# Attention in one fused layer: two heads' scores in the two halves of TensorE's rows, in float32r parts, and row maxima of two heads by one VectorE instruction

## The chip, the cores and the metric

The kernel runs on one core of a Trainium2 chip. The metric is the device time of one execution in microseconds (us). The profiler's record of one execution is a span from its first to its last instruction.

## The reference

One layer with gated cross-attention and a gated mixture of experts, all in float32, with B=4, S=512, D=256, 16 heads of 16, 8 experts of which each token takes 2, and a shared expert of width 512:

```
q = split_heads(layernorm(x) @ Wq.T + bq);  k, v = split_heads(ctx @ Wk.T + bk), split_heads(ctx @ Wv.T + bv)
attn = softmax(einsum('bhqd,bhkd->bhqk', q, k) / 4)
x = x + tanh(g_xattn) * (merge_heads(einsum('bhqk,bhkd->bhqd', attn, v)) @ Wo.T + bo)
x = x + tanh(g_ffn) * (moe(layernorm(x)) + (silu(h @ gate_w) * (h @ up_w)) @ down_w)
```

## The kernel before, in words

The program is written engine by engine: each engine's block is a list of instructions in program order, with semaphores between the engines. Nothing reorders them.

**Projections.** For each batch `b`, TensorE makes the value rows (`value_rows`) and four tiles of 128x512 of k and q (`chunk(b, j)`; j 0 and 1 are k, 2 and 3 are q). A score needs more digits than a bf16 product has, so every tile of q and k is cut into three bf16 parts: ScalarE writes the first (`first_part`), VectorE the float32 remainder (`rest`), ScalarE the second part (`second_part`), GpSimd the third (`third_part`). SyncE stores the parts in DRAM (`store_parts`) and loads them back (`load_group`) so that the 16 rows of a head stand six times above each other, as the six pairs of parts in `Q_PART` and `K_PART`: 96 partitions of QS (queries) and KST (keys) for one head, four heads side by side. A bf16 product over these 96 rows sums the six partial products.

**Groups.** Four heads of a batch are a group; there are 16 groups (`GROUPS`), each of four steps `kt` (a tile of 128 keys). A step of group i has on TensorE, in this order: scores of heads 0 and 1 (L1523, keys in the partitions, queries along 512 columns), one product for the maxima (L1305, `scores_for_max`, queries in the partitions), scores of head 2, a second product for the maxima, in step 2 the transpose of the finished maxima (`max_transpose`, L1315), the product with the values of the step before (`values`, L1395: four heads in four column tiles of 32, two instructions each), a third product for the maxima, scores of head 3, a fourth product for the maxima. The maxima run six heads ahead (`smax_schedule`); they end with step 1 of group 14. In the last six steps pieces of the output projection and of the next stage (`tail`) stand at the end of each step.

**The softmax.** exp needs minus the row maximum, which is added by the score product itself: rows 96 and 97 of QS hold minus the maximum in two bf16 parts, the same rows of KST hold ones (a GpSimd memset for each b, `kones`). VectorE takes each 128x512 product's maxima (L842, `one_max`), TensorE turns the 128x16 tile into PSUM bank 7, ScalarE copies the first part (`m_first`, L676), VectorE subtracts for the second (`m_second`, L853), and two DMAs bring them into QS (`load_max`, L360). ScalarE applies exp to each score tile (L730) and, once a group, copies the group's output (`out_copy`, L718).

**PSUM.** Banks 0 to 2 are the ring of the scores, 3 to 5 the ring of the maxima, 6 holds the output, 7 the turned maxima and a bias product. A score product waits until exp has read the bank three tiles before; a maxima product waits for the reduction three tiles before.

**SyncE.** In group i it loads the first four of the six terms of group i+3 (8 DMAs, after the scores of group i-1), the maxima of group i+1 (2 DMAs), the other two terms (4 DMAs), and three small transfers of softmax sums and scales.

Of the kernel before, what the change touches and what calls it, by code (L numbers as in the profile page):

```python
# [5 lines left out]
P = 128  # L6
# [4 lines left out]
BF16 = mybir.dt.bfloat16  # L11
# [4 lines left out]
def flamingo_layer(nc, x, ctxT, g_xattn, g_ffn, WqT, bq, WkT, bk, WvT, bv, WoT, bo,  # L16
# [16 lines left out]
    TERMS = 6  # L33
    Q_PART = [0, 1, 2, 0, 1, 0]
    K_PART = [0, 0, 0, 1, 1, 2]
# [18 lines left out]
    q_scr = nc.dram_tensor("q_parts", (B, 3, D, S), BF16, kind="Internal").ap()  # L54
    k_scr = nc.dram_tensor("k_parts", (B, 3, D, S), BF16, kind="Internal").ap()
# [9 lines left out]
    with ExitStack() as stack:  # L65
# [6 lines left out]
        def sems(name, n):  # L72
# [30 lines left out]

        R1 = sb("R1", [P, 8192])
# [10 lines left out]
        REST = R3[:, 0:2048].rearrange("p (j n) -> p j n", j=4)  # L115
        QP = R3[:, 5120:8192].bitcast(BF16).rearrange("p (j a n) -> p j a n", j=4, a=3)

        QS = [R1[:, 1024 * g:1024 * (g + 1)].bitcast(BF16).rearrange("p (h n) -> p h n", h=G) for g in range(NG)]
        KST = [R1[:, 4096 + 1024 * g:4096 + 1024 * (g + 1)].bitcast(BF16).rearrange("p (h n) -> p h n", h=G)
               for g in range(NG)]  # L120
# [4 lines left out]
        mparts = sb("mparts", [G * TB, 2, 2, P], BF16)  # L125
# [79 lines left out]
        q1_ready, q2_ready, q3_ready = (sem(n) for n in ("q1_ready", "q2_ready", "q3_ready"))  # L205
        rest_ready = sem("rest_ready")
# [7 lines left out]
        smax_done, max_ready = sem("smax_done"), sem("max_ready")  # L214
        mt_done, m1_ready, m2_ready = sem("mt_done"), sem("m1_ready"), sem("m2_ready")
        m_in = sems("m_in", 2)
        st_done, exp_done, pv_done, ot_ready = sem("st_done"), sem("exp_done"), sem("pv_done"), sem("ot_ready")
# [44 lines left out]

        def smax_schedule(i, kt):

            s = 4 * i + 6 + kt
            return s if s < GROUPS * G else None

        OUT_AT = TB + 1
        M2_AT = 2 * TB + 1
# [11 lines left out]
        def bank(kind, b, part=0):  # L281
            return 3 + USERS.index((kind, b, part)) % 3

        def gu_bank(n, k):
# [4 lines left out]
            return (2, 6)[k] if n < IC + 2 else 2 + k  # L289
# [7 lines left out]
        def smax_bank(n):  # L297
# [4 lines left out]
            return (6, 4, 5)[n % 3] if n < EARLY else 3 + n % 3  # L302

        def max_user(n):

            users = [m for m in range(n) if smax_bank(m) == smax_bank(n)]
            return users[-1] + 1 if users else 0
# [12 lines left out]
        def _(sp):  # L320
# [14 lines left out]
            def store_parts(b):  # L335
                for j in range(4):
                    dst = k_scr if j < 2 else q_scr
                    sp.wait_ge(q3_ready, 4 * b + j + 1)
# [7 lines left out]
            def load_group(i, terms=range(TERMS)):  # L346
# [1423 lines left out]
```

## Time and profile before

| | us |
|---|---|
| median of 3 executions | 469.4 (468.83 to 470.41) |
| span of the profiled execution | 466.8 |
| TensorE busy in it | 453.6 (97%) |
| VectorE busy | 331.8 (71%) |
| ScalarE busy | 252.6 (54%) |
| GpSimd busy | 154.4 (33%) |

The profiled execution's own time isn't given apart from its span. Busy time of TensorE is modelled and counts a product until its end has drained, so a product that follows another closely overlaps it in the rows: what a product takes of a stream is read from the distance of two starts, not from its duration. PE is TensorE's matmul, PEld its weight load, DVE is VectorE, ACT ScalarE, POOL GpSimd, SPq the DMA queue of SyncE. The tensors R1 to R4 appear as R, PSUM as PS.

### The profile page before, as it was taken

The page shows a single profiled execution, that of the slowest core. Times are in us where ns is not written, and L with a number is a line of the kernel's source. Part 1 is how long each engine was busy: PE and PEld are TensorE (multiplying, and loading weights), DVE is VectorE, ACT ScalarE, POOL GpSimd, SP SyncE. Part 2 cuts the span into 40 slices and gives each one's busy share as a digit, 9 for nine tenths or more (in the row PEclk, how much of TensorE's full clock was granted, in tenths as well). Part 3 has the DMA queues.
Part 4 walks back from the last instruction along what each step waited for, and adds up shares of the span by engine and source line. Part 5 has one row for each costly group of instructions (what it writes and reads, how often), then busy time and mean ns, then how long its engine had stood idle before and what let it go on. Part 6 is the DMA issues. An engine that isn't in the chain of part 4 may idle for free.

```text
span 466.8 us, 8100 instructions
## 1 busy us (share of the span) xinstructions
PE 453.6 (97%) x2310; PEld 215.8 (46%) x2310; DVE 331.8 (71%) x841; ACT 252.6 (54%) x540; POOL 154.4 (33%) x209
## 2 busy tenths in 40 slices
PE   8999999999999999999999989889999999999997
PEld 8664432222222222222465634565555555555745
DVE  1988898888888888888578766354565656532674
ACT  2664477777777777777565111023666766631110
POOL 5493488111212121212132766600323332332000
PEclk9999999999999999999999999979999999999999
DMA  8669762335353535353548522311322222312921
GB/s 261 223 181 251 157 204 58 86 83 97 90 98 94 98 94 97 95 92 102 167 135 264 211 91 81 110 48 46 93 84 88 85 88 83 90 49 60 377 101 47
DMA packets 54140, 56.71 MB, mean 121 GB/s; under 512 B 13456, under 2 KB 44560, under 8 KB 54096
## 3 DMA queue, kind: packets, MB, share of 16 engines
q1 hardware_dynamic: 47504, 43.82, 34.1%
q0 software_dynamic: 4960, 10.53, 7.4%
q10 hardware_dynamic: 1632, 1.84, 1.2%
q8 instruction: 20, 0.33, 0.3%
q14 instruction: 24, 0.20, 0.2%
HBM read 36.35 MB, written 17.72 MB: 116 GB/s over the span
## 4 chain that ended last, share of the span: by engine, by line
PE 90%; DVE 4%; issue 2%; DMA 1%; SPq 1%; another core or an unknown queue 1%; POOL 1%; ACT 1%; DVEq 0%; POOLq 0%
PE PS L1395 13%; PE PS L1305 13%; PE PS L1523 12%; PE PS L1567 11%; PE PS L1677 9%; PE PS L1580 6%; PE PS L1696 5%; PE PS L1357 4%; PE PS L1672 3%; PE PS L1442 3%; PE PS L1691 2%; PE PS L1651 2%; DVE nmax L842 2%; PE PS L1335 2%; PE PS L1659 2%
## 5 line engine op out<-in xcount | busy, mean ns | idle before, releaser
L842 DVE TENSOR_REDUCE nmax<-PS 128x1 f32<-128x512 f32 x256 | 159.4, 683 | 21.4 <-PE PS L1305 21.4
L730 ACT ACTIVATE R<-PS 128x512 f32<-128x512 f32 x256 | 134.1, 601 | 42.0 <-PE PS L1523 41.7
L1305 PE MATMUL PS<-R 96*128 96x512 bf16 x256 | 96.1, 382 | 1.2 <-DMA R<-k_parts 1.0
L1523 PE MATMUL PS<-R 98*128 98x512 bf16 x256 | 86.2, 380 | 0.3 <-DVE R L860 0.3
L1395 PE MATMUL PS<-R 128*32 128x512 f32 x512 | 68.2, 604 | 0.0
L621 POOL DMA_INDIRECT token_y<-R,dest x34 | 32.6, 960 | 93.4 <-DVE R L1184 92.0
L1305 PEld LDWEIGHTS PS<-R 96*128 96x128 bf16 x256 | 24.8, 97 | 69.7 <-DVE nmax L842 51.1
L1677 PE MATMUL PS<-R 128*128 x100 | 47.3, 595 | 0.2 <-ACT R L798 0.2
L745 ACT ACTIVATE R<-PS 128x512 f32<-128x512 f32 x16 | 9.6, 597 | 68.7 <-PE PS L1567 52.1
L600 POOL DMA_DIRECT2D CH<-R x56 | 27.4, 496 | 54.4 <-ACT R L718 54.4
L1523 PEld LDWEIGHTS PS<-R 98*128 98x128 bf16 x256 | 24.8, 97 | 38.6 <-ACT R L730 22.6
L1222 DVE TENSOR_TENSOR R<-R,PS 128x256 f32<-128x256 f32 x34 | 14.3, 421 | 33.3 <-issue 19.7
L575 POOL DMA_INDIRECT slot_x<-CH,pos x32 | 31.1, 972 | 13.7 <-issue 8.7
L568 POOL TENSOR_TENSOR CH<-CH,w_v 128x512 f32<-128x512 f32 x7 | 8.9, 1265 | 77.7 <-DMA w_v<-o_scales 77.7
L1567 PE MATMUL PS<-R,wup 128*128 128x512 f32 x64 | 32.0, 625 | 1.5 <-issue 1.5
L1567 PE MATMUL PS<-R,wgate 128*128 128x512 f32 x64 | 30.7, 596 | 2.0 <-issue 2.0
L1580 PE MATMUL PS<-wdown,R 128*128 128x256 f32 x128 | 29.7, 388 | 0.0
L795 ACT ACTIVATE R<-PS 128x256 f32<-128x256 f32 x34 | 13.0, 383 | 29.7 <-PE PS L1677 26.3
L1580 PEld LDWEIGHTS PS<-wdown,R 128*128 128x128 f32 x128 | 24.8, 196 | 5.2 <-issue 2.0
L1696 PE MATMUL PS<-fc,R 128*128 x100 | 25.6, 380 | 0.0
L1677 PEld LDWEIGHTS PS<-R 128*128 128x128 f32 x100 | 18.7, 190 | 14.3 <-issue 13.1
L533 POOL TENSOR_TENSOR R<-R 128x512 bf16<-128x512 f32 x16 | 18.5, 1160 | 18.2 <-ACT R L669 18.1
(177 smaller groups left out, 598.4 us busy)
## 6 DMA issues: line engine op xcount, KB each, us to landing
R<-q_parts SPq DMA_DIRECT2D x96, 64.0 KB, 3.1
R<-k_parts SPq DMA_DIRECT2D x96, 64.0 KB, 3.1
R<-in_fc_w_dram SPq DMA_DIRECT2D x16, 256.0 KB
R<-token_y SPq DMA_DIRECT2D x4, 1024.0 KB, 9.0
R<-slot_x SPq DMA_DIRECT2D x25, 129.0 KB
k_parts<-R SPq DMA_DIRECT2D x8, 384.0 KB, 3.3
q_parts<-R SPq DMA_DIRECT2D x8, 384.0 KB, 3.5
fc<-in_fc_w_dram SPq DMA_DIRECT2D x16, 128.0 KB
```

The source lines that it names most:

```text
L575: nc.gpsimd.indirect_dma_start(slot_x, bass.IndirectOffsetOnAxis(ap=pos[:, t, k:k + 1], axis=0), CH[:, t, :], None).then_inc(scattered, 16)
L600: pool.dma_start(CTX[at:at + DK, i // 2, :], OT[i % 2][P // G * j:P // G * j + DK, :]).then_inc(ctx_in[i % 2], 16)
L621: nc.gpsimd.indirect_dma_start(token_y, bass.IndirectOffsetOnAxis(ap=dest[:, j:j + 1], axis=0), YE[:, j % UN, :], None).then_inc(y_out[j % ...
L730: nc.scalar.activation(PT[:, kt, j, :], PS[:, (G * (TB * i + kt) + j) % 3, :], ACT.Exp).then_inc(exp_done, 1)
L842: nc.vector.tensor_reduce(nmax[:, i % 2, j * TB + qt:j * TB + qt + 1], PS[:, smax_bank(n), :], AX.X, ALU.max, negate=True).then_inc(max_re ...
L1305: mm(PS[:, smax_bank(n), :], QS[g][0:KS, j, qt * P:(qt + 1) * P], KST[g][0:KS, j, :], start=True, stop=True).then_inc(smax_done, 1)
L1395: last = mm(PS[32 * j:32 * j + VW, 6, :], VA[:, b * TB + kt, (g * G + j) * VS:(g * G + j) * VS + VW], PT[:, kt, j, :], start=(kt == 0), st ...
L1523: mm(PS[:, n % 3, :], KST[g][0:KM, j, kt * P:(kt + 1) * P], QS[g][0:KM, j, :], start=True, stop=True).then_inc(st_done, 1)
L1567: last = mm(PS[:, gu_bank(n, k), :], w[:, d, c * P:(c + 1) * P], H2T[:, d, b * S:(b + 1) * S], start=(d == 0), stop=(d == DC - 1))
L1580: last = mm(PS[:, down_bank(b, t), half * D:(half + 1) * D], HS[:, b % 2, c, t * P:(t + 1) * P], wdown[:, c, :], start=(c == 0 and half == ...
L1677: last = mm(PS[:, 1 + u, :], XGT[:, u, c * P:(c + 1) * P], fc1[:, c, e, :], start=(c == 0), stop=(c == DC - 1))
L1696: last = mm(PS[:, 5 + u, 0:D], HET[:, u, c * P:(c + 1) * P], fc2[:, c, e, :], start=(c == 0), stop=(c == IE // P - 1))
```

## The change

1. **Parts.** q and k are cut into two parts in place of three: the high part is rounded to float32r by ScalarE, the low part is the float32 remainder that VectorE writes at once. `second_part` and `third_part` go. Three pairs of parts (high-high, low-high, high-low) in place of six: 48 rows for one head, 50 with the two rows of maxima, and both operands are float32r.
2. **Halves.** Heads 0 and 2 of a group stand in partitions 0 to 49, heads 1 and 3 in 64 to 113. A product takes one of the two halves of the rows.
3. **Maxima.** The products for the maxima alternate between the halves and use banks 4 to 7 in pairs; one VectorE instruction reduces two banks (128x2x512) to two columns. The first 24 are still reduced one by one.
4. **Turned maxima.** VectorE splits the 128x16 maxima before the transpose (`split_max`, two small instructions); TensorE turns both parts at once into a bank of the scores' ring (turn 11 of a group's 17), and ScalarE copies them out with one instruction (`max_rows`), after the exp of step 2, head 2. Both DMAs of `load_max` follow it.
5. **Order.** In a step: scores 0 and 1, maxima 0 and 1, scores 2, transpose, values, scores 3, maxima 2 and 3. Output bank 6 becomes 3; later users of 3 to 5 take 4 to 6.
6. The ones in KST are whole-tile memsets at the start, and a group's loads wait for them. `bias_row` stands before VectorE's first step.

```
-    TERMS = 6
-    Q_PART = [0, 1, 2, 0, 1, 0]
-    K_PART = [0, 0, 0, 1, 1, 2]
+    TERMS = 3
+    Q_PART = [0, 1, 0]
+    K_PART = [0, 0, 1]
+    UNIT = 2 * TERMS
+    HALF = P // 2
...
-    q_scr = nc.dram_tensor("q_parts", (B, 3, D, S), BF16, kind="Internal").ap()
+    q_scr = nc.dram_tensor("q_parts", (B, 2, D, S), F32, kind="Internal").ap()
...
+        MT_AT = 2 * G + 3
+        def score_turn(i, kt, j):
+            return (G * TB + 1) * i + G * kt + j + (i + 1 < GROUPS and G * kt + j >= MT_AT)
+        def max_turn(i):
+            return (G * TB + 1) * (i - 1) + MT_AT
...
-            return (6, 4, 5)[n % 3] if n < EARLY else 3 + n % 3
+            return (6, 4, 5)[n % 3] if n < EARLY else 4 + (n - EARLY) % 4
...
-            def load_group(i, terms=range(TERMS)):
+            def load_group(i, pieces=range(UNIT)):
...
+                else:
+                    sp.wait_ge(kones, g + 1)
...
+                for piece in pieces:
+                    t, r = divmod(piece, 2)
+                    at = slice(HALF * r + t * DK, HALF * r + (t + 1) * DK)
+                    sp.dma_start(QS[g][at, :, :].bitcast(F32),
+                                 q_scr[b, Q_PART[t], rows, :].rearrange("(h r d) n -> r d h n", r=2, d=DK)[r])\
+                      .then_inc(ld_group[g], 16)
...
             def load_max(i):
-                for part, s in ((0, m1_ready), (1, m2_ready)):
-                    sp.wait_ge(s, i + 1)
+                sp.wait_ge(m_ready, i + 1)
+                for part in range(2):
+                    sp.dma_start(QS[i % NG][KS + part:P:HALF, :, :].bitcast(F32).rearrange("p h n -> p (h n)"),
+                                 mparts[G * TB * part:G * TB * (part + 1), i % 2, :]).then_inc(m_in[i % 2], 16)
...
+            def two_max(n):
+                i, _, at = max_tile(n)
+                for r in range(2):
+                    dve.wait_ge(smax_done[r], n // 2 + 1)
+                nc.vector.tensor_reduce(nmax[:, i % 2, at:G * TB:G * TB // 2], PS[:, smax_bank(n):smax_bank(n) + 2, :], AX.X,
+                                        ALU.max, negate=True).then_inc(max_ready, 1)
+            def split_max(i):
+                dve.wait_ge(max_ready, maxima(G * TB * (i + 1)))
...
+                nc.vector.tensor_copy(nmax_parts[:, i % 2, 0, :].bitcast(F32R), nmax[:, i % 2, :]).then_inc(high_max, 1)
+                dve.wait_ge(high_max, i + 1)
+                nc.vector.tensor_tensor(nmax_parts[:, i % 2, 1, :], nmax[:, i % 2, :], nmax_parts[:, i % 2, 0, :],
+                                        ALU.subtract).then_inc(split_ready, 1)
...
+            bias_row()
             for i in range(GROUPS):
                 for kt in range(TB):
...
+                    t = smax_schedule(i, kt)
+                    for h in range(2):
+                        if t is not None:
+                            two_max(TB * t + 2 * h)
+                        if kt == 1 and h == 1 and i + 1 < GROUPS:
+                            split_max(i + 1)
...
             def max_transpose(i):
+                pe.wait_ge(split_ready, i + 1)
+                if i:
+                    turn_free(max_turn(i))
...
-                    mm(PS[:, n % 3, :], KST[g][0:KM, j, kt * P:(kt + 1) * P], QS[g][0:KM, j, :],
-                       start=True, stop=True).then_inc(st_done, 1)
+                    turn = score_turn(i, kt, j)
+                    turn_free(turn)
+                    h, r = divmod(j, 2)
+                    at = slice(HALF * r, HALF * r + KM)
+                    mm(PS[:, turn % 3, :], KST[g][at, h, kt * P:(kt + 1) * P], QS[g][at, h, :],
+                       start=True, stop=True).then_inc(st_done[r], 1)
...
                     mx[0]()
+                    mx[1]()
                     scores(kt, 2)
-                    mx[1]()
...
+                    scores(kt, 3)
                     mx[2]()
-                    scores(kt, 3)
                     mx[3]()
```

## Rows read from the trace of the kernel before

**Rows 1.** Chain that ended last, the page: shares of the span.
```profile
PE 90%; DVE 4%; issue 2%; DMA 1%; SPq 1%; another core or an unknown queue 1%; POOL 1%; ACT 1%; DVEq 0%; POOLq 0%
```
**Rows 2.** Busy time by stretch: stretch, length, busy (count) by engine, clock, DMA, GB/s.
```profile
139.90:151.40 11.50, 11.50 (x69) 3.23 (x65) 10.27 (x19) 8.89 (x18) 3.19 (x5) 1.00 0.38 91
```
**Rows 3.** Timeline, one step of group 6: start, us, engine, line, what [idle before].
```profile
140.15 0.38 PE L1523 MATMUL PS<-R 98*128 98x512 bf16 x1
...
140.35 2.48 DVE L842 TENSOR_REDUCE nmax<-PS 128x1 f32<-128x512 f32 x4 [0.36 <-PE PS L1305]
140.37 0.38 PE L1305 MATMUL PS<-R 96*128 96x512 bf16 x1
...
140.57 2.06 ACT L730 ACTIVATE R<-PS 128x512 f32<-128x512 f32 x4 [0.78 <-PE PS L1523]
...
141.22 0.10 PEld L1523 LDWEIGHTS PS<-R 98*128 98x128 bf16 x1 [0.31 <-ACT R L730]
...
141.46 0.38 PE L1305 MATMUL PS<-R 96*128 96x512 bf16 x1
...
141.77 1.06 PE L1395 MATMUL PS<-R 128*32 128x512 f32 x8
...
142.77 0.39 PE L1305 MATMUL PS<-R 96*128 96x512 bf16 x1
```
**Rows 4.** Timeline, the values' product one group later.
```profile
153.28 1.07 PE L1395 MATMUL PS<-R 128*32 128x512 f32 x8
```
**Rows 5.** Groups of instructions, whole span: busy, mean ns | idle before, releasers.
```profile
L842 DVE TENSOR_REDUCE nmax<-PS 128x1 f32<-128x512 f32 x256 | 159.4, 683 | 21.4 <-PE PS L1305 21.4
L730 ACT ACTIVATE R<-PS 128x512 f32<-128x512 f32 x256 | 134.1, 601 | 42.0 <-PE PS L1523 41.7
L1184 DVE COPY R<-PS 128x256 f32<-128x256 f32 x34 | 14.4, 424 | 11.7 <-PE PS L1696 7.2 <-PE PS L1691 2.8
L955 DVE COPY R<-PS 128x512 f32<-128x512 f32 x4 | 2.7, 686 | 2.0 <-remote 1.9
L1017 DVE TENSOR_TENSOR PRE<-PRE,OHS 128x8 f32<-128x8 f32 x16 | 2.7, 167 | 0.5
```
**Rows 6.** Timeline of SyncE's queue, one round of DMA issues.
```profile
153.60 0.46 SPq L352 DMA_DIRECT2D R<-q_parts  x1
...
159.48 1.29 SPq L360 DMA_DIRECT2D R<-mparts  x2
...
164.06 0.58 SPq L376 DMA_DIRECT2D w_v<-o_scales  x1
```
**Rows 7.** DMA issues: count, size, median us to landing.
```profile
R<-mparts SPq DMA_DIRECT2D x32, 4.0 KB, 2.3
```
**Rows 8.** Timeline of TensorE ahead of the first group.
```profile
16.76 3.70 PE L1357 MATMUL PS<-R,w_q 128*128 128x512 f32 x8
20.30 1.04 PE L1282 MATMUL PS<-ident,R 128*128 128x128 f32 x8
...
36.95 0.61 PE L1305 MATMUL PS<-R 96*128 96x512 bf16 x2 [0.98 <-DMA R<-k_parts]
...
53.62 0.27 PE L1315 MATMUL PS<-ident,nmax 128*16 128x128 f32 x1
```
**Rows 9.** Timeline of VectorE, ScalarE and GpSimd around the first group's start.
```profile
59.66 0.74 DVE L860 SCALAR_TENSOR_TENSOR R<-PS,bias_sc,R 128x512 f32<-128x512 f32 x1
60.44 0.62 ACT L669 CAST R<-R 128x512 bf16<-128x512 f32 x1 [1.00 <-DVE R L860]
62.38 0.93 POOL L551 TENSOR_SCALAR tg_bo<-bo_row,tg 128x256 f32<-128x256 f32 x1
```
**Rows 10.** Timeline of TensorE in one of the last six steps.
```profile
236.50 0.81 PE L1523 MATMUL PS<-R 98*128 98x512 bf16 x3
237.25 1.06 PE L1395 MATMUL PS<-R 128*32 128x512 f32 x8
```

More of the change, by code:

```diff
@@ L10 @@
 F32 = mybir.dt.float32
-BF16 = mybir.dt.bfloat16
+F32R = mybir.dt.float32r
 U32 = mybir.dt.uint32
@@ L101, in flamingo_layer @@
         minus_half = sb("minus_half", [P, NT])
+        with nc.sbuf_tensor("QK", [P, 8192], F32R) as QK:
+            pass
         R1 = sb("R1", [P, 8192])
@@ L261, in flamingo_layer, with max_tile, maxima @@
         EARLY_J = ((0, 0, 0, 0), (0, 0, 0, 0), (2, 2, 2, 2), (2, 2, 2, 2))
+        def max_tile(n):
+            i, m = divmod(n, G * TB)
+            h, m = divmod(m, 2 * TB)
+            qt, r = m // 2, m % 2
+            return i, (h, r, qt), 2 * TB * r + TB * h + qt
+        def maxima(tiles):
+            return min(tiles, EARLY) + max(tiles - EARLY, 0) // 2
+        MT_AT = 2 * G + 3
[3 more added lines that the diff above has]
+            return (G * TB + 1) * (i - 1) + MT_AT
         def smax_schedule(i, kt):
@@ L288, in gu_bank @@
                 return k
-            return (2, 6)[k] if n < IC + 2 else 2 + k
+            return 2 + k
         def down_bank(b, t):
@@ L675, in m_first @@
                     act.wait_ge(m_in[i % 2], 32 * (i // 2))
-                nc.scalar.copy(mparts[:, i % 2, 0, :], PS[0:G * TB, 7, 0:P]).then_inc(m1_ready, 1)
+                nc.scalar.copy(mparts[:, i % 2, :], PS[0:2 * G * TB, max_turn(i) % 3 if i else 7, 0:P]).then_inc(m_ready, 1)
             def load_context(b):
@@ L893, in _ @@
                 for j in range(4):
-                    if b == B - 1 and j == 2:
-                        m_second(0)
+                    if b == B - 1 and j == 1:
+                        split_max(0)
                     early_max(EARLY_J[b][j])
@@ L898, in _ @@
             early_max(EARLY - sum(map(sum, EARLY_V + EARLY_J)))
-            def head_max(s):
-                for qt in range(TB):
-                    one_max(TB * s + qt)
             def scale_of(i):
@@ L953, in h2t_second @@
                 dve.wait_ge(h2_t, 2 * b + 2)
-                dve.wait_ge(st_done, G * TB * (GROUPS - 1 + b // 2))
+                for r in range(2):
+                    dve.wait_ge(st_done[r], G // 2 * TB * (GROUPS - 1 + b // 2))
                 nc.vector.tensor_copy(H2T[:, 1, b * S:(b + 1) * S], PS[:, bank("h2_t", b, 1), :]).then_inc(h2t_ready[1], 1)
```

203 lines of the change are left out of this document (82 added, 121 removed).

## Prediction

> **What bounds the kernel now.** I read first the chain that ended last: 90% of it is TensorE [rows 1]. The busy table of one group (11.50 us, four steps) shows TensorE without a gap, VectorE at 10.27 us, ScalarE at 8.89 us, at the full granted clock of 2.4 GHz [rows 2]. So in groups 0 to 14 a step takes what TensorE's stream takes. The timeline has the parts: a bf16 product follows the next after 0.22 us (140.15, 140.37), the values start 0.31 us after the last product before them (141.46 to 141.77), and the next product 1.00 us after they start (to 142.77) [rows 3]. Eight products and the values: 7 x 0.22 + 0.31 + 0.99 = 2.84 us. Four such steps and the transpose (0.14 more) are 11.51 us, the distance of two values' products a group apart (141.77, 153.28) [rows 3, 4]. VectorE has 0.36 us idle a step, ScalarE 0.78 us [rows 3]: neither is far behind.
>
> **The products.** A float32r product isn't in the trace. Its bounds: a bf16 one costs 0.22 us of the stream [rows 3]; a float32 one of 512 columns stands as two instructions of 0.44 us each (eight from 16.76 to 20.30) [rows 8], 0.88 us in all, four times the bf16 price, as of four narrow partial products. One product of parts that are already narrow is one of these four: I take 0.22 us; 0.44 us (float32 operands streamed as slowly as there) and 0.88 us are the ends. Weight loads don't hold it up: float32 loads of 128 columns keep a pace of 0.11 us with their products ((1.04 - 0.28) / 7) [rows 8], and two loads stand to one 0.22 us of a pair.
>
> That two halves of the rows work side by side isn't in the trace either. Its nearest row is the values: eight instructions of column tiles, which end to end would be 8 x 0.44 = 3.5 us, take 1.00 us [rows 3, 8]. Bounds for a pair: 0.22 us (side by side) and 0.44 us (one after the other). I take side by side. In the new order every two neighbours are of different halves, or the third follows in the half that comes free, so eight products take 4 x 0.22 = 0.88 us where they took 1.75 us. TensorE's own work in a step falls from 2.84 to about 2.0 us. That isn't the new step: TensorE waits in program order, and the other limits are near.
>
> A switch between the values' column tiles and whole rows costs the trace little: 0.09 us before the values (0.31 - 0.22) and 0.14 us after them (1.00 less two passes of 0.43) [rows 3]; the new order has the same two switches a step and one more at the transpose. TensorEngine Tiling in the Trainium skill (Key Properties) says that a change of tiling mode drains the engine, and that speaks against this change, whose products are in a third mode. By that rule the sum would be the drain rival's below; by the row it stays as it is.
>
> **The new step.** The products of step kt, the values of kt-1 and exp form a ring. After the values only scores 3 can start; head 2 of the next step uses the bank of scores 3, and the next values need its exp. So: values 0.99, scores 3 to the start of exp 0.42 (140.15 to 140.57), exp 0.58 (its four take 2.06, at 0.49 from start to start), 0.07 to TensorE (the first exp ends 141.15, the load starts 141.22), scores 2 and the switch 0.31 [rows 3]: 2.37 us. In place of 2.84 us, and set by latencies, not by work.
>
> VectorE: a reduction of 512 columns takes 0.683 us, 0.60 from start to start ((2.48 - 0.68) / 3) [rows 3, 5]. Copies from PSUM of 256 and 512 columns (424 and 686 ns) give 1.02 ns a column [rows 5], so 1024 columns take 0.68 + 0.52 = 1.21 us, 1.13 from start to start, 2.26 us a step against 4 x 0.60 = 2.40 now. It fits under 2.37 us, and `two_max` alone gains little. ScalarE: 4 x 0.49 = 1.96 us a step. Once a group `out_copy` comes ahead of the exp of step 0, head 3: it can start only when the last values have ended, takes 0.50 us, and pushes that exp by about 0.22 us.
>
> **The wait that the change adds.** `split_max` needs all sixteen maxima of the next group, the last of which come from the second pair of step 1. From the start (0) of that step's values: maxima 3 is issued at 1.21 us, can be read at 1.63, VectorE reads it until 2.84, then its two small instructions, which wait for the one before each: 2 x 0.17 (nearest row, 128x8 columns) + 0.08 = 0.42 us [rows 5]. TensorE may transpose at 3.33 us and starts the next values at 3.64 us, 1.27 us later than 2.37. Before, the transpose needed one reduction less and no split, and lay in 0.14 us. Behind the waiting transpose on TensorE stand the values and scores 3; exp runs dry meanwhile. The transpose also takes a turn of the ring, and ScalarE copies 128 columns in 0.25 us or less, behind an exp: no further cost that I can see.
>
> Group: 4 x 2.37 + 0.22 + 1.27 = 10.97 us, against 11.51: **-0.54 us**. Over groups 0 to 13 and half of 14: 14.5 x -0.54 = **-7.8 us**.
>
> **The transfers.** SyncE issues 17 DMAs a group, 12 of them loads of the same number and size. It is at it from 153.60 to 164.64 us with a pause only ahead of the maxima (157.4 to 159.48) [rows 6]: 9.0 us of 10.97, no bound. The maxima's DMAs are issued behind exp and copy, about 1.4 us after the transpose, and land 0.6 + 2.3 = 2.9 us later [rows 6, 7], 4.3 us after it; the next group's scores come a step, the values and the rest after it: also about 4.3 us. Taken as nothing; 0.3 us a group (4 us in all) if it lands late.
>
> **Ahead of the groups.** The chain to the first loads loses ScalarE's and GpSimd's parts, some 1.8 us, so the wait of 0.98 us at 36.95 goes; ten pairs of early maxima could save 0.22 us each; the first transpose (53.62), issued at once before, waits for a split, 0.5 us [rows 8]. Between -0.98 - 2.2 + 0.5 = -2.7 and 0; since VectorE and the banks wait for each other there, I take **-1.5 us**. Stores grow from 384 to 512 KB; nothing waits for them but the reuse of QP. `bias_row` now stands ahead of VectorE's first pair and waits for tanh and GpSimd's 0.93 us, which come after the last part of q: VectorE is free at about 59.7, ready at 60.2 [rows 9]: **+0.5 us**.
>
> **The last six steps** are TensorE's work (out projection): scores 0 to 2 took 0.22 each (236.50, 0.81 for three with the end, then values at 237.25) [rows 10]; one of them falls beside another: 6 x -0.22 = **-1.3 us**. What follows shifts with it.
>
> **Sum:** -7.8 - 1.5 + 0.5 - 1.3 = -10.1 us. The profiled span of 466.8 us becomes 456.7; the median lies 2.6 us above that span, so the time is **459.3 us**. Split at 0.17 or 0.7 us, side costs of 0.3 us a group and the early bounds give 450 to 468 for this case.
>
> **The rivals.**
> - *Forecast* (halves side by side at 0.22 us): 0.60.
> - *No wait at the transpose.* If VectorE isn't late, the 1.27 us shrink to the transpose's 0.3 us: 14.5 x -0.97 = -14, 445 us. Against it: the order of the instructions. 0.07.
> - *The halves don't run side by side (the other side).* Then TensorE's work stays 2.84 us a step, and the new order adds the split's wait at the transpose, 0.83 us more a group than now (I follow the same chain with 0.22 us for each product: 12.34 us): 14.5 x 0.83 = +12, and none of the early and late savings: 481 us. It decides once a pair takes over about 0.3 us in place of 0.22. For it: no row of the trace shows row tiles; against it: the column tiles. 0.13.
> - *Half rate,* 0.44 us a product side by side: 12.48 us a group, 483 us; TensorE is then as full as before. 0.07. FP8 and Floating Point Precision in the Trainium skill (TensorE Precision Notes) names four passes for float32 and one read of reduced precision beside it, which speaks against; no row here shows it.
> - *Full price,* 0.88 us: over 18 us a group, 570 us. 0.03.
> - *Drains.* If each switch with the half-row mode costs 0.1 us more, nine a group, group 11.8 us: +0.3 x 14.5 = +4, less the early and late 2.3: 471 us. The page's rule; the switches in the trace are against it. 0.08.
> - Anything else (a late load, the clock falling in the new waits): 0.02.
>
> **How the numbers follow.** Faster is the forecast, the first rival and the edge of the drains; no measurement of this kernel tells less than 0.3% from no change. Faster 0.68, same 0.05, slower 0.27. The forecast's own range is 450 to 468; to hold 8 in 10 it has to reach over the drains to the edge of the serial halves: 448 to 481.
>
> **What the next profile would show.** Two products of one pair starting within some tens of ns, 0.22 us between pairs; `two_max` at 1.21 us; values 2.4 us apart in plain steps and 3.6 us around the transpose; the transpose's weight load idle some 1 us behind the split; the first score of a group not waiting for `mparts`; groups at 11.0 us. Starts 0.22 us apart within a pair, or a duration of 0.6 us for a product, make it wrong.

## The result, and the profile after

The changed kernel takes 482.8 us (median of 4 runs, 479.4 to 489.3) where the kernel before takes 469.1 us (467.0 to 470.4) on the same chip: a ratio of 1.028, 95% interval 1.022 to 1.034. **It is slower.** The prediction was 459.3 us, 448 to 481: wrong in sign, and the time lies outside the range. Ratios in this document leave out runs more than 1.5% above the fastest of their kernel, which had a lower granted clock (here the one of 489.3 us); medians hold all runs. The profiled execution took 481.0 us, with a span of 479.3 against 466.8.

The page of the kernel after: the busy shares, the granted clock in 40 slices, the chain (its line for before is in [rows 1]), and two groups of instructions.
```profile
PE 449.7 (94%) x2310; PEld 231.2 (48%) x2310; DVE 326.5 (68%) x741; ACT 246.7 (51%) x524; POOL 132.4 (28%) x193
...
PEclk9999988999999999999989999989999999999999
...
PE 80%; DVE 10%; issue 3%; ACT 2%; DMA 2%; another core or an unknown queue 1%; POOL 0%; ACTq 0%; DVEq 0%; POOLq 0%
...
L865 DVE TENSOR_REDUCE nmax<-PS 128x2 f32<-128x1024 f32 x116 | 137.9, 1221 | 26.1 <-PE PS L1320 26.1
...
L1548 PEld LDWEIGHTS PS<-QK 50*128 50x128 f32 x256 | 42.6, 188 | 80.9 <-ACT R L742 61.9
```
TensorE's share of the chain fell from 90% to 80% and VectorE's rose from 4% to 10%: TensorE waits for VectorE now.

The timeline of the step ahead of the transpose and of the transpose itself, one group of the kernel after; [rows 3] is the step of before.
```profile
140.75 1.06 PE L1418 MATMUL PS<-R 128*32 128x512 f32 x8
...
141.75 0.18 PEld L1548 LDWEIGHTS PS<-QK 50*128 50x128 f32 x1 [0.84 <-ACT R L742]
141.75 0.49 PE L1548 MATMUL PS<-QK 50*128 50x512 f32 x1
...
141.75 0.73 PE L1320 MATMUL PS<-QK 48*128 48x512 f32 x2
...
142.28 2.06 ACT L742 ACTIVATE R<-PS 128x512 f32<-128x512 f32 x4 [0.53 <-PE PS L1548]
...
142.59 1.23 DVE L865 TENSOR_REDUCE nmax<-PS 128x2 f32<-128x1024 f32 x1 [0.18 <-PE PS L1320]
...
143.85 0.17 DVE L873 CAST nmax_parts<-nmax 128x16 fp32r<-128x16 f32 x1
144.05 0.17 DVE L875 TENSOR_TENSOR nmax_parts<-nmax,nmax_parts 128x16 f32<-128x16 f32 x1
...
144.28 0.28 PE L1337 MATMUL PS<-ident,nmax_parts 128*32 128x128 f32 x1 [0.87 <-DVE nmax_parts L875]
...
144.50 1.07 PE L1418 MATMUL PS<-R 128*32 128x512 f32 x8
```
The halves do run side by side: scores 3 and a maxima product both start at 141.75. But exp starts 0.53 us behind the scores (forecast 0.42), and the plain steps that follow, values at 144.50, 147.10 and so on, are 2.61 us long where 2.37 was forecast. The transpose waits 0.87 us; from the values at 140.75 to those at 144.50 it is 3.75 us (forecast 3.64). Three plain steps, 0.07 for `out_copy` and 3.75 make 11.65 us, against 11.51 before.

Some groups are longer. Timeline of the kernel after beside GpSimd's scaling of the context:
```profile
154.88 1.26 POOL L588 TENSOR_TENSOR CH<-CH,w_v 128x512 f32<-128x512 f32 x1 [12.90 <-DMA w_v<-o_scales]
155.50 0.67 DVE L873 CAST nmax_parts<-nmax 128x16 fp32r<-128x16 f32 x1
...
156.43 0.28 PE L1337 MATMUL PS<-ident,nmax_parts 128*32 128x128 f32 x1 [1.35 <-DVE nmax_parts L875]
```
The cast takes 0.67 us instead of 0.17, and TensorE waits for all of it. The first split inside the loop meets other work of GpSimd, additions of 128x256 tiles from 64.55 to 75.56 us, and both of its instructions are slow:
```profile
70.81 0.67 DVE L873 CAST nmax_parts<-nmax 128x16 fp32r<-128x16 f32 x1
71.52 0.65 DVE L875 TENSOR_TENSOR nmax_parts<-nmax,nmax_parts 128x16 f32<-128x16 f32 x1
```
And TensorE's clock falls to the lower of its two levels where it did not before. Busy time by stretch (columns as in [rows 2]), kernel after; then one of these stretches in the kernel before:
```profile
62.00:66.00 4.00, 3.04 (x14) 1.21 (x12) 3.73 (x7) 2.59 (x5) 2.77 (x12) 1.00 0.67 230
66.00:70.00 4.00, 4.00 (x19) 1.83 (x19) 2.58 (x3) 2.21 (x5) 4.00 (x6) 0.61 1.01 365
70.00:74.00 4.00, 2.23 (x15) 0.72 (x15) 3.23 (x4) 1.38 (x4) 4.00 (x7) 0.93 0.04 14
74.00:78.00 4.00, 4.00 (x22) 1.65 (x19) 2.36 (x2) 2.31 (x5) 1.56 (x3) 0.61 0.02 4
```
```profile
66.00:70.00 4.00, 3.85 (x25) 1.19 (x27) 3.70 (x8) 3.06 (x8) 3.78 (x9) 1.00 0.93 311
```
A granted clock of 0.61 over 4 us is mostly 1.2 GHz. TensorE had waited (busy 3.04 of 4 us) ahead of it.

**Where 12.5 us of span went**, by the starts of values in both timelines: the first values come at 66.58 instead of 63.77 (+2.8); those behind the first transpose of the loop at 72.43 instead of 67.03 (+2.6 more); 14 groups later 239.50 instead of 228.13 (+6.0: 14 x 0.14 = 2.0, four slow splits beside GpSimd 2.6, and 1.2 in the first of these groups, part of which ran at half clock); the last values at 268.36 instead of 253.52 (+3.5); after them 210.9 us instead of 213.3 (-2.3; from 300 to 330 us the granted clock is 0.94 instead of 0.89).

### The profile page after: what moved, and what is told of

It is laid out like the page before. It is cut to its first block, busy times and chain, and to the rows that moved or that the text cites. A ratio compares the mean times of both kernels' runs of the same rounds, so it can differ in the third digit from the quotient of the medians.

```text
span 479.3 us, 8092 instructions
## 1 busy us (share of the span) xinstructions
PE 449.7 (94%) x2310; PEld 231.2 (48%) x2310; DVE 326.5 (68%) x741; ACT 246.7 (51%) x524; POOL 132.4 (28%) x193
## 4 chain that ended last, share of the span: by engine, by line
PE 80%; DVE 10%; issue 3%; ACT 2%; DMA 2%; another core or an unknown queue 1%; POOL 0%; ACTq 0%; DVEq 0%; POOLq 0%
PE PS L1418 14%; PE PS L1590 12%; PE PS L1548 11%; PE PS L1700 9%; PE PS L1603 6%; PE PS L1320 5%; PE PS L1719 5%; DVE nmax L865 4%; PE PS L1380 3%; PE PS L1465 3%; PE PS L1695 3%; ACT R L742 2%; PE PS L1714 2%; PE PS L1674 2%; DMA X<-in_x_dram 2%
## 5 line engine op out<-in xcount | busy, mean ns | idle before, releaser
L865 DVE TENSOR_REDUCE nmax<-PS 128x2 f32<-128x1024 f32 x116 | 137.9, 1221 | 26.1 <-PE PS L1320 26.1
L1548 PE MATMUL PS<-QK 50*128 50x512 f32 x256 | 94.2, 455 | 1.8 <-ACT R L742 0.5
L1548 PEld LDWEIGHTS PS<-QK 50*128 50x128 f32 x256 | 42.6, 188 | 80.9 <-ACT R L742 61.9
L1320 PE MATMUL PS<-QK 48*128 48x512 f32 x256 | 78.3, 449 | 0.4 <-DVE nmax L865 0.2
L1418 PE MATMUL PS<-R 128*32 128x512 f32 x512 | 69.6, 616 | 0.0
L1320 PEld LDWEIGHTS PS<-QK 48*128 48x128 f32 x256 | 34.6, 187 | 13.8 <-DVE nmax L851 5.4
L794 ACT COPY R<-R 128x512 f32 x36 | 20.7, 629 | 4.7 <-issue 4.7
```

What stands on the lines that cost most here:

```text
L865: nc.vector.tensor_reduce(nmax[:, i % 2, at:G * TB:G * TB // 2], PS[:, smax_bank(n):smax_bank(n) + 2, :], AX.X, ALU.max, negate=True).then ...
L1320: mm(PS[:, smax_bank(n), :], QS[g][at, h, qt * P:(qt + 1) * P], KST[g][at, h, :], start=True, stop=True).then_inc(smax_done[n % 2], 1)
L1418: last = mm(PS[32 * j:32 * j + VW, 3, :], VA[:, b * TB + kt, (g * G + j) * VS:(g * G + j) * VS + VW], PT[:, kt, j, :], start=(kt == 0), st ...
L1548: mm(PS[:, turn % 3, :], KST[g][at, h, kt * P:(kt + 1) * P], QS[g][at, h, :], start=True, stop=True).then_inc(st_done[r], 1)
```

## The experiments

Chips differ: before took 469.0, 459.6, 468.2 and 471.1 us in the four sessions. So each time is read against before in its own session.

**1. Products alone.** The layer is left out; TensorE runs series of ten products of each kind, and the output is not the layer's.
```
for _ in range(10):
    mm(PS[:, 0, :], FR[0:96, 0:P], FR[0:96, 512:1024]); values()       # L73, the float32 values L67
...
for _ in range(10):
    mm(PS[:, 0, :], BF[0:50, 0:P], BF[0:50, 512:1024])                 # L113
    mm(PS[:, 5, :], FF[:, 0:P], FF[:, 512:1024])                       # L114, a whole float32 product
```


> Leaves the whole layer out: it only issues series of TensorE products on the same tiles and writes a part of x as output. Each series is ten rounds. Values means the kernel's product with the values (four column tiles of 32, float32, 512 columns), 0.99 to 1.00 us of the stream. One product in front of the values, round by round: bf16 over 96 rows 1.31 us (the trace of before). Theory A (the cost is in the switch to a tile of 64 rows: the engine drains and cannot load ahead): float32r over 96 rows also 1.31 to 1.35, bf16 over 50 rows and float32r over 50 rows both about 1.53. Theory B (the cost is in float32r, whose weights are not loaded ahead): float32r over 96 rows and over 50 rows both about 1.53, bf16 over 50 rows 1.31. Streams: bf16 and float32r over 96 rows 0.22 us a product, halves of the rows in turn 0.11 us a product, float32r on one half alone 0.22. Between whole float32 products of 0.86 us: bf16 over 96 rows adds 0.22, a 50-row product adds 0.41 (early part of the changed kernel) by theory A whatever its type. Eight float32r products in the two halves and the values: 0.88 + 1.0 + 0.2 to 0.3 = 2.1 to 2.2 us; eight bf16 products and the values 2.84.

Timeline of TensorE in this kernel: bfloat16 of 96 rows between values; float32r of 96; bfloat16 of 50 rows; last, float32r pairs of two halves.
```profile
15.44 0.39 PE L69 MATMUL PS<-BF 96*128 96x512 bf16 x1
...
16.76 0.39 PE L69 MATMUL PS<-BF 96*128 96x512 bf16 x1
...
33.12 0.50 PE L73 MATMUL PS<-FR 96*128 96x512 f32 x1
...
34.55 0.50 PE L73 MATMUL PS<-FR 96*128 96x512 f32 x1
...
43.32 0.39 PE L77 MATMUL PS<-BF 50*128 50x512 bf16 x1
...
44.64 0.39 PE L77 MATMUL PS<-BF 50*128 50x512 bf16 x1
...
83.66 0.39 PE L97 MATMUL PS<-FR 50*128 50x512 f32 x1
83.66 0.39 PE L98 MATMUL PS<-FR 50*128 50x512 f32 x1
83.89 0.39 PE L97 MATMUL PS<-FR 50*128 50x512 f32 x1
```
The period with the values is 1.32 us (16.76 - 15.44), 1.43 and 1.32, and 1.43 for float32r of 50 rows. What costs 0.11 us is float32r, not the half rows (theory B, with half of its 0.22 us); and the record of such a product is 0.50 us long instead of 0.39. In a stream float32r keeps 0.23 us a product and a pair of halves takes the same 0.23 (83.66 to 83.89): it is only at the start behind another kind that a product is late. Between whole float32 products it is otherwise. The same kernel, lines 105, 109, 113 and 117 beside whole float32 products:
```profile
90.83 0.38 PE L105 MATMUL PS<-BF 96*128 96x512 bf16 x1
...
91.90 0.38 PE L105 MATMUL PS<-BF 96*128 96x512 bf16 x1
...
113.37 0.39 PE L113 MATMUL PS<-BF 50*128 50x512 bf16 x1
...
114.74 0.39 PE L113 MATMUL PS<-BF 50*128 50x512 bf16 x1
...
127.44 0.50 PE L117 MATMUL PS<-FR 50*128 50x512 f32 x1
...
128.92 0.49 PE L117 MATMUL PS<-FR 50*128 50x512 f32 x1
```
1.07 us with 96 rows, 1.37 with 50, 1.48 with 50 in float32r (float32r of 96 rows: 1.09). Here the half-row tile costs 0.30 us (0.39 in float32r), as theory A has it. And eight float32r products in the two halves with the values take 2.12 us a round, eight bfloat16 products of 96 rows with the values 2.83: TensorE's own work does fall as forecast.

**2. Parts cut to bfloat16.** The products of scores and maxima read the upper 16 bits of each part, so the scores are rounded.
```
-  mm(..., KST[g][at, h, kt * P:(kt + 1) * P], QS[g][at, h, :], ...)
+  mm(..., KST[g][at, h, kt * P:(kt + 1) * P].bitcast(bfloat16)[:, 1:2 * P:2],
+     QS[g][at, h, :].bitcast(bfloat16)[:, 1:2 * S:2], ...)
```


> Edit: the changed kernel, but the products of the scores and of the maxima read the upper 16 bits of each float32 part as bfloat16 (the parts are cut to 8 bits, so the scores are rounded; nothing else is changed, the half rows, the pairs, the reductions and the order stay). Theory (the plain step of 2.61 us is 0.22 longer than forecast because a float32r product that starts behind another kind or behind a wait first shows 0.11 us of its weight load, twice in the ring): the values start 1.00 - 0.11 = 0.89 to 0.91 us ahead of scores 3 or the first exponential starts 0.42 us behind scores 3 instead of 0.53, and scores 2 to values takes 0.31 instead of 0.42, so the plain step is 2.39 us; the transpose step stays at 3.7 us, since VectorE sets it, and a group is 3 x 2.39 + 3.75 = 10.9 us instead of 11.65. Rival (it is the change between half-row tiles and the values' column tiles that costs the time): the plain step stays at 2.61 us and the group at 11.65.

Timeline of one step of this kernel:
```profile
84.78 1.07 PE L1419 MATMUL PS<-R 128*32 128x512 f32 x8
85.78 0.40 PE L1549 MATMUL PS<-QK 50*128 50x512 bf16 x1
...
86.21 2.06 ACT L742 ACTIVATE R<-PS 128x512 f32<-128x512 f32 x4 [0.35 <-PE PS L1549]
...
86.86 0.40 PE L1549 MATMUL PS<-QK 50*128 50x512 bf16 x1
87.19 1.07 PE L1419 MATMUL PS<-R 128*32 128x512 f32 x8
```
Scores 3 to exp 0.43 us (0.53 in the changed kernel), scores 2 to values 0.33 (0.42): the plain step is 2.41 us (84.78 to 87.19), and a group 11.07. The whole takes 461.8 us, one run, where before takes 459.6. So the two terms of the ring that were short are shown, 0.10 us each. The group is 3 x 2.41, 0.19 for `out_copy`, and 3.64 around the transpose; the 0.17 us over the 10.9 expected are `out_copy`, which the expectation had left out. The recorded prediction's group of 10.97 us is met within 0.1 us.

The kernel still isn't faster than before. From its second transpose in the loop to its last (82.15 to 231.12 us) a group takes 11.46 us on average: three splits meet GpSimd's product (the transpose waits 1.68 to 2.00 us), and four groups' first scores wait 0.28 to 0.94 us for the turned maxima.

**3. Transpose behind the values of its step.**
```
                     scores(kt, 2)
-                    if kt == 2 and i + 1 < GROUPS:
-                        max_transpose(i + 1)
                     if kt: values(i, kt - 1) ...
+                    if kt == 2 and i + 1 < GROUPS:
+                        max_transpose(i + 1)
```


> The transpose of the maxima stands behind the values of step 2 in place of ahead of them. My theory (the wait for VectorE's last reduction and the split holds up the values, the ring values, scores 3, exp, scores 2 sets the rest): the values of step 2 start 2.6 us after those of step 1 in place of 3.75, the transpose waits under 0.2 us, a group takes 10.9 us in place of 11.65 (the ring is longer by the transpose, 0.2 to 0.3 us), 14 groups give 10 us: about 472 us. Rival (VectorE is the bound, the wait only shows it): the wait moves to the next maxima products and a group stays above 11.5 us, 480 us or more. Second rival (the maxima's DMAs land too late now that the group is shorter): the first scores of a group wait for the DMA by some 0.5 to 1 us, 478 us.

479.3 us (474.7 to 483.7), 1.020 of before (1.009 to 1.030). The waits at the transpose are gone but for one of 0.20 us, and groups of 10.72 us appear, but in three groups the next scores wait 1.65 to 1.76 us for the turned maxima: the second rival, with a longer wait. Timeline of one group in which they don't wait and the next, in which they do:
```profile
127.08 1.12 SPq L388 DMA_DIRECT2D QK<-mparts  x2
...
129.64 0.64 PE L1548 MATMUL PS<-QK 50*128 50x512 f32 x2
...
137.81 1.12 SPq L388 DMA_DIRECT2D QK<-mparts  x2
...
142.40 0.50 PE L1548 MATMUL PS<-QK 50*128 50x512 f32 x2 [1.65 <-DMA QK<-mparts]
```
The same two transfers landed within 2.6 us of their issue in one group and 4.6 us in the next. Behind one such wait the clock was 0.50 for 12 us and more (190 to 202 us).

**4. The same, and four loads behind the turned maxima's transfers.** In addition to the edit of 3:
```
-  load_group(i + 3, range(0, UNIT - 2)); load_max(i + 1); load_group(i + 3, range(UNIT - 2, UNIT))
+  load_group(i + 3, range(0, UNIT - 4)); load_max(i + 1); load_group(i + 3, range(UNIT - 4, UNIT))
```


> Edit: the changed kernel with the turning of the maxima behind the values of its step (the edit of the run before) and, new, four of each group's loads of parts moved behind the turned maxima's two transfers on SyncE's queue, so that those transfers have no pieces of 64 KB running ahead of them. Theory (in the run before, the turned maxima landed 4.4 us after their issue in every second group, because their 512-byte rows ran in between the pieces still under way, and 2.5 us in the others): no scores product waits for mparts any more, every group but those beside the scaling of the context takes 10.7 us, the span is 475.4 - 5.2 of waits - some 4 us that the lower clock behind one of these waits cost = 466 us, the time about 469 us. Rival (the transfers are late through GpSimd's stores, whatever the order on SyncE): waits of 1.6 to 1.8 us stay in every second group, and the time is that of the run before, 479 us. Second rival (the pieces moved back land too late for the maxima of their group): waits of TensorE for k_parts or q_parts at L1320 appear in most groups, and groups are over 11 us.

**453.2 us (451.7 to 454.5) where before takes 459.6: 0.986 (0.982 to 0.990).** Timeline of this kernel:
```profile
93.46 0.28 PE L1337 MATMUL PS<-ident,nmax_parts 128*32 128x128 f32 x1
...
104.19 0.28 PE L1337 MATMUL PS<-ident,nmax_parts 128*32 128x128 f32 x1
```
From the first transpose in the loop on, groups take 10.72 us, to a few hundredths, those beside GpSimd's scaling too, with no wait of the product for the turned maxima. The gain is shown, though it is under 2%. The span, 451.2 us, isn't to be set against 466.8: this chip is faster, by some 9.5 us for the kernel before.

**5. Again, in five rounds,** without an edit.

> No edit: once more the kernel with the transpose behind the values and four of each group's loads behind the turned maxima's transfers, in five rounds. It took 0.986 of before on a chip on which before took 459.6 us; with the 12 extra products it took 0.991 on a chip on which before took 468.2 us. Theory (the gain is the groups' 0.79 us x 14 = 11 us, less 2.8 us ahead of the groups, 0.7 to 3 in the first group at half clock and 3.2 in the last six steps, and is there on every chip): ratio 0.985 to 0.992 and, in the profile, groups of 10.72 us without a wait for the turned maxima, last values 4 to 6 us sooner than 253.5. Rival (the gain belongs to that one chip): ratio 0.995 or more.

467.1 us (463.7 to 469.8) against 471.1: 0.993 (0.989 to 0.996). The last values start at 249.69 us, 3.8 us sooner than in before; groups are 10.72 us, with some a little longer. Both intervals lie below 1, so the gain doesn't belong to one chip. It came out smaller where the profiled execution had more stretches at the lower clock (mean granted clock 0.978 against 0.996); that the clock is the reason is argued, not shown.

**6. The changed kernel again,** on the chip of the second kernel of experiment 11.

> No edit: the changed kernel once more, on the chip on which the two edits on its queues are compared. Theory (the two edits to the order take 0.93 us from each group and nothing else): this kernel is at 1.02 to 1.033 of before, as in its first comparison, 470 to 474 us where before takes 459.6, and its profile has groups of 11.65 us and more, with a span 16 to 20 us above 451.2: 14 x 0.93 = 13.0 from the groups, some 2.5 to 4 from the casts beside GpSimd's scaling and the rest from stretches of lower clock. Rival (the chip, not the order, made the last kernel fast): this kernel is within 1% of before here.

485.8 us, 1.035 of before (1.030 to 1.040). The rival (within 1% of before) is out, and the ratio lies a little above the 1.02 to 1.033 expected. The chip is not the one of experiment 4: before takes 468.2 us here, so the 470 to 474 us expected can't be compared. Undisturbed groups are 11.65 us again; the granted clock was 0.51 from 68 to 88 us and 0.53 from 184 to 194.

**7. GpSimd scales 8 columns instead of 512** (most of the context goes unscaled): `CTX[:, n, 0:8]` and `SCALES[:, 0:8]`.

> Edit: the changed kernel, but GpSimd scales 8 columns of each context tile instead of 512 (so most of the context goes unscaled). Theory (the casts of the maxima take VectorE 0.67 to 1.18 us instead of 0.17 where GpSimd's 1.26 us product of two SBUF tiles runs at the same time): the groups of 12.15 and 12.6 us go, every undisturbed group is 11.65 us, the transposes wait 0.86 us and none 1.3 or 1.8, and the span falls by about 2.5 to 3 us if nothing else moves. Rival (these casts are late for another reason, for instance DMA traffic): single casts of 0.6 us and more stay and so do the longer groups.

Timeline at the place where the changed kernel's transpose waited 1.35 us:
```profile
154.91 0.20 POOL L588 TENSOR_TENSOR CH<-CH,w_v 128x8 f32<-128x8 f32 x1 [13.82 <-DMA w_v<-o_scales]
155.06 0.28 PE L1337 MATMUL PS<-ident,nmax_parts 128*32 128x128 f32 x1 [0.86 <-DVE nmax_parts L875]
```
Every transpose from the second group of the loop on waits 0.85 to 0.87 us, every one of those groups is 11.65 us but for a few hundredths. GpSimd's product is what lengthened the later splits. The first transpose in the loop still waits 1.77 us, beside GpSimd's additions, which this edit leaves as they are. The single run, 470.0 us, is on the chip on which before takes 459.6: 1.023.

**8. Reductions over half the columns** (the maxima are those of 256 of 512 columns): `PS[:, ...:... + 2, 0:S // 2]`.

> The pair reductions read 256 of each 512 columns, so the maxima are those of half the keys: VectorE's instruction falls from 1.22 to about 0.70 us. My theory (the ring of values, scores, exp and values sets a plain step): plain steps stay at 2.61 us, only the wait at the transpose shrinks by 0.5 us, a group falls from 11.65 to about 11.1. Rival (VectorE's reductions bound the step): four steps of 2 x 0.52 less, a group of 10 us or under.

A reduction takes 0.69 us, the transposes wait 0.33 us instead of 0.87, the plain steps are 2.61 us (values at 95.53 and 98.14), and a group is 11.13 us instead of 11.65. So VectorE bounds the transpose and not the plain step. 476.2 us, one run, on the chip of experiment 3.

**9. Two reductions of one bank in place of one over two banks.**
```
-  tensor_reduce(nmax[... two columns ...], PS[:, bank:bank + 2, :], ...)
+  tensor_reduce(nmax[... first ...], PS[:, bank, :], ...)
+  tensor_reduce(nmax[... second ...], PS[:, bank + 1, :], ...)
```


> Edit: the changed kernel, but two reductions of one bank each (0.68 us each) take the place of one over two banks (1.22). Theory (the reductions do not bound the plain step, but their end sets the transposes' wait): plain steps stay at 2.61 us; the last pair of maxima ahead of the split ends about 0.15 us later in each of the two reductions that follow one another, so the transpose waits 1.0 to 1.2 us instead of 0.86 and a group takes 11.8 to 12.0 us. Rival (VectorE is what holds the plain steps as well): plain steps grow to 2.75 us (four reductions of 0.68) or more, and a group to over 12.2 us.

Timeline: values of the plain steps, and the transpose.
```profile
93.41 1.07 PE L1419 MATMUL PS<-R 128*32 128x512 f32 x8
...
96.02 1.07 PE L1419 MATMUL PS<-R 128*32 128x512 f32 x8
...
102.31 0.09 PEld L1338 LDWEIGHTS PS<-ident,nmax_parts 128*32 128x32 f32 x1 [1.23 <-DVE nmax_parts L876]
102.31 0.28 PE L1338 MATMUL PS<-ident,nmax_parts 128*32 128x128 f32 x1 [0.92 <-ACT R L742]
```
The plain step stays 2.61 us; the transpose waits 0.92 us and a group is 11.72, less than the 11.8 expected. The view names an exp for the product's wait, but the second instruction of the split ends at 102.25 us, and the transpose's own weight load names it. `two_max` gains 0.07 us a group and no more. The single time, 494.0 us, is not read as the edit's price: the granted clock was 0.955 on average (0.50 from 66 to 82 us, where the first transpose waited 4.57 us).

**10. The ones ahead of the first root.** GpSimd's four memsets of K's banks come first, not between its two powers and beside VectorE's normalisation.

> GpSimd writes the ones into the whole KST tiles before its first root instead of behind the second, where VectorE's normalisation of x runs. My theory: the normalisation of batches 1 and 2 takes 1.4 us a batch in place of 2.8, TensorE no longer waits at 26.4 us, and the first values come 0.3 to 0.5 us earlier: 482 us, 0 to 1 us under the changed kernel, which can't be told from no change. The 2.8 us by which the first values came late are in the switches to the half-row tiles between the whole float32 products, which stay. Rival (the late start is the ones' work): all of it goes, 479.5 us.

484.6 us, 1.032 of before (1.025 to 1.038): no gain. The normalisation of four tiles is back at 1.38 us (2.86 in the changed kernel, from 16.94 us, beside memsets from 16.85), yet the first values start 0.8 us later than there (67.42). The traces of the two kernels show where. The first projection product starts at 7.71 us instead of 6.94, a start that lies at 6.79 in experiment 4 and 7.10 in experiment 2, whose instructions are the same up to there; whether the edit has a part in it is not shown. By the transposes of the third batch the lag of 0.77 us is 0.37 (26.80 and 26.43 us; TensorE's wait of 0.23 us for VectorE is gone), so from there the edit gave back 0.4 us, within the 0.3 to 0.5 expected. The lag then stays to the scores (63.19 and 62.84 us), and the other 0.5 us is the clock, granted at 0.76 from 64 to 66 us and 0.50 behind that. So most of VectorE's 1.5 us was not on the path.

**11. Extra products against the lower clock,** alone and with the two edits of 4: each maxima product of the loop's first three steps is issued twice into its bank (12 more products).

> Edit: the changed kernel, but in the first three steps of the group loop each product of the maxima is issued twice into the same bank (12 extra products, no result changed), so that TensorE waits less between 62 and 72 us. Theory (the granted clock of 0.61 and 0.50 between 66 and 78 us follows the stretch in which TensorE was busy only 3.0 of 4 us): with the stretch filled the clock stays at 1.00, values 0 take 1.07 us instead of 1.72, and the transpose of the first group starts 2 to 3 us sooner than at 72.22; span about 2.5 us less. Rival (the clock falls for another reason, such as the transfers of over 300 GB/s in the same 4 us): the clock is still 0.50 to 0.6 in 66 to 70 us, and the 12 products only add up to 1.4 us.

> Edit: the two edits of the fastest kernel so far (transpose behind the values of its step; four of each group's loads behind the turned maxima's transfers) and the 12 extra maxima products of the first three steps. Theory (in that kernel the clock was still granted at 0.57 between 66 and 70 us, the values there took 1.83 us instead of 1.07, and the stretch ahead of it had TensorE busy 3.1 of 4 us; with the extra products the clock stayed at 1.00 there, and its transpose does not wait the 1.8 us that brought the clock down one stretch later): the clock is 1.00 from 62 to 82 us, the first group's transpose starts at 70.5 to 71 us instead of 72.0, span 1 to 1.5 us less than 451.2, ratio to before 0.983 to 0.986. Rival (the extra products cost as much as the clock gives back): span 451 to 452, ratio 0.986 to 0.99. Groups stay at 10.72 us in both.

Alone: 471.6 us, one run, where before takes 459.6. Busy time by stretch with the 12 products:
```profile
66.00:70.00 4.00, 3.78 (x26) 1.87 (x25) 3.23 (x4) 2.91 (x7) 4.00 (x7) 1.00 1.03 382
70.00:74.00 4.00, 2.25 (x11) 0.37 (x11) 2.77 (x4) 1.12 (x3) 4.00 (x7) 0.68 0.18 64
```
The clock stays at 1.00 in the first stretch, with the same transfers (382 GB/s), so they alone don't lower it; but the first transpose waits 1.81 us and the clock falls behind that wait. Nor is TensorE's wait ahead of the stretch enough by itself: in the kernel of experiment 2 it was busy 3.07 of the 4 us from 62 to 66, and the clock stayed at 1.00 from 66 to 70. With the two edits of 4: 467.9 us (median of 12 runs, 461.4 to 471.1) where before takes 468.2. The ratio of 0.991 (0.987 to 0.995) is of the seven runs up to 468.2 us; the medians of all runs show no gain. In its profile the clock was at 0.51 in 66 to 70 us in spite of the extra products (TensorE busy 3.47 of the 4 us ahead). They are worth nothing that shows, and which wait brings the clock down in which run stays open.

## Why the prediction was wrong

**The products: right.** 0.22 us was taken for a float32r product and for a pair of halves; they measure 0.23 both. FP8 and Floating Point Precision in the Trainium skill (TensorE Precision Notes), cited against the half rate, gives no price but names four passes for float32 and one read of reduced precision; 0.23 us against 0.86 for a whole float32 product of 512 columns fits that.

**"Weight loads don't hold it up": this is the step that failed.** It rested on the pace of a row of eight products of one kind [rows 8]. In a series the pace hides the load; at the head of a series, where a product starts behind another kind or behind a wait, it doesn't. A float32r load takes 0.18 to 0.19 us (bfloat16 0.10), and such a product is 0.11 us later there than a bfloat16 one. That it is the load, and not something else at the start of a float32r product, is argued from these lengths; the runs show the 0.11 us and that it goes with the type of the operands. The ring has two heads: scores 3 behind the values (exp 0.53 later, not 0.42) and scores 2 behind its wait for exp (values 0.42 later, not 0.31). The plain step is 2.37 + 0.11 + 0.11 = 2.59 us, measured 2.61. Shown by the series (1.43 against 1.32 us) and by the cut parts (2.41 us). At three steps a group, 0.72 us: more than the whole forecast gain of 0.54. In the kernel of experiment 2 the group gets back 0.58 us (11.65 to 11.07), since `out_copy` then costs 0.19 us again. This is the largest part of the miss, 14 x 0.72 = 10 of the 22.6 us between the forecast span and the measured one. It isn't all of it: that kernel, without this cost, took 461.8 us where before takes 459.6. The other parts follow.

**The wait at the transpose: mechanism right,** 3.75 us against 3.64. `split_max` cost its 0.42 us, and the shorter reductions (experiment 8) took 0.54 us off the wait. `out_copy` costs 0.07 us, not 0.22 (0.19 in the shorter ring of experiment 2). Group: 10.97 + 0.72 + 0.11 - 0.15 = 11.65.

**VectorE's two small instructions at 0.17 us: right where they stand alone,** but four groups met GpSimd's product of two SBUF tiles and paid 0.2 to 0.95 us for it (2.6 us in all; experiment 7), and the first split in the loop, beside GpSimd's additions, took 1.0 us more (no run takes these additions away). No term had it. Before, VectorE had no such instruction in front of the transpose, but its trace has a small instruction that is slow in the same way. Timeline of the kernel before, VectorE on 128x4 elements (0.17 us elsewhere) while GpSimd writes a third part from 20.05 to 21.21 us:
```profile
20.45 0.79 DVE L825 TENSOR_SCALAR var_eps<-mv 128x4 f32<-128x4 f32 x1
```

**Ahead of the groups: wrong sign.** -1.5 + 0.5 was forecast, +2.8 measured. At 44 us the kernel after is 0.4 us ahead (value rows from 44.35 instead of 44.73), and the wait for the parts [rows 8] is gone. Then each of the maxima's pairs, which have whole float32 products on both sides, stands in a period of 2.34 us with its chunk instead of 2.16: the 0.22 us saved by the pair are less than what the switch takes. A single one has a period of 1.49 instead of 1.09, as in the series (1.48 against 1.07). With the parts cut to bfloat16 (experiment 2) the two periods are 2.24 and 1.39 and the first values start at 65.49 us, so 0.1 us of each goes with float32r and the rest with the half rows. From 44 to 60 us all this is +2.6 us with the first transpose's wait of 0.41 and its switches. Here the rule that was weighed and set aside has its say: TensorEngine Tiling in the Trainium skill (Key Properties) has the engine drain at a change of tiling mode, and beside whole rows the half rows did cost 0.30 us more. Beside the values' column tiles they cost nothing more (1.32 us with 50 rows and with 96), and those are the switches of the ring. `bias_row` came as forecast, as far as it shows: first scores to first values 4.45 us instead of 4.00.

**The clock,** in "anything else" at 0.02, took about 1.0 of the 2.6 us to the first transpose's values: that step is 5.85 us long here and 4.82 in the first kernel of experiment 11, where the clock stayed at 1.00 over it and the split was slow as well; another 1.0 is the slow split and 0.5 the new step itself (3.75 against 3.26). It took 1.2 us in the next group and 1.7 us behind the last transpose (values 7.41 us apart, 5.74 in the kernel with the 12 products, which was at full clock there; granted 0.72 from 240 to 246 us). Each such stretch comes behind one in which TensorE waited (0.96 us in 62 to 66 us, 0.86 us at the last transpose), but most waits of 0.86 us have none behind them.

**The last six steps: -1.3 forecast, +3.5 measured:** 1.7 of it the clock, 1.8 six steps that are 0.25 to 0.32 us longer each. With the parts cut to bfloat16 the six steps take 26.1 us, against 25.4 in the kernel before and 27.2 with float32r at full clock (the kernel with the 12 products): 1.1 of the 1.8 us goes with float32r. That the other 0.7 is the half rows beside whole products is argued from the series, not shown.

**The rivals.** The time lies where the serial halves were put (481), by another way: the halves run side by side. The drains' sum (471) had the price in the wrong place. The wait at the transpose, which the first rival had gone, can go: with the transpose moved and the transfers in order the group is 10.72 us, and the kernel is faster than the changed one and, by 0.7 to 1.4%, than the one before.

## What to carry to other kernels

Price a product at the head of a series apart from one within it: in a ring set by latencies its later start is on the path at each head. Where an instruction must wait for another engine, put it behind work that is ready, and then look at what its result feeds: here the transfers became late until fewer loads stood ahead of them. Small instructions that now lie on the path want a look at what GpSimd does at that moment, and the trace of before may already show what that costs.

## What was not expected of the hardware

- A float32r product of 512 columns: 0.23 us in a series, 0.11 us late at its head; its weight load of 128 columns 0.18 to 0.19 us, where the bfloat16 one stands at 0.10.
- A half-row product between whole float32 products costs 0.30 us more than one of 96 rows, beside the values' column tiles nothing.
- VectorE's cast or subtraction of 16 columns took 0.41 to 1.12 us instead of 0.17 beside GpSimd's product of two SBUF tiles (up to 1.23 in experiment 2), and its normalisation of four tiles 2.86 us instead of 1.38 beside GpSimd's memsets.
- Two transfers of 8 KB on one queue landed within 2.6 us of their issue in one group and 4.6 us in the next.
- One kernel took 459.6 us on one chip and 471.1 on another, 11.5 us apart, where the whole change made 13.7.
